# The two value products of a decoder block: stationary operands of 32 columns in four column tiles in place of 64 in two

## The reference, cut to what matters

```
# causal linear attention, q and k already turned and made positive by phi
num = einsum('bhd,bhde->bhe', q_t, sum over s <= t of k_s v_s)
den = max(einsum('bhd,bhd->bh', q_t, sum over s <= t of k_s), 1e-6)
y = num / den

# cross attention, Q = norm(x), K = V = ctx
attn = softmax(einsum('bhqd,bhkd->bhqk', Q, K) / sqrt(8))
context = einsum('bhqk,bhkd->bhqd', attn, V)
```

## Time and profile before

| | |
|---|---|
| runs, median (lowest to highest) | 1055.57 us (1054.49 to 1060.03), 3 runs |
| the profiled execution | 1064.24 us, its span 1062.0 us |
| TensorE: matmul busy, load busy | 863.1 us (81%), 695.8 us (66%) |
| VectorE, ScalarE, GpSimd busy | 730.3 us, 583.0 us, 598.8 us |
| mean granted TensorE clock | 0.926 of full speed |
| blocks of a_values, of b_values | 64 each, from 32.2 and 91.3 us on, the last at 597.9 and 666.4 us |

### The profile page before, as it was taken

How to read it: one execution, slowest core, us unless ns; L and a number is a source line. 1 busy time by engine, 2 the same in 40 slices (tenths; PEclk the granted TensorE clock), 3 DMA queues, 4 the chain that set the end, 5 groups by cost and what they waited for, 6 DMA issues and landing times.

```text
span 1062.0 us, 27434 instructions
## 1 busy us (share of the span) xinstructions
PE 863.1 (81%) x9293; PEld 695.8 (66%) x9294; DVE 730.3 (69%) x1980; ACT 583.0 (55%) x1116; POOL 598.8 (56%) x792
## 2 busy tenths in 40 slices
PE   4779989898888988898888875987988898888810
PEld 3567777677677776677766654876866676666610
DVE  2346768878887888787798986667555555555545
ACT  3567658667666667666766553532355555545410
POOL 4455435865766666676585665247066666665620
PEclk9789889999998999999999987898999999999965
DMA  9011011111101101102101103111122222222169
GB/s 250 2 41 41 2 41 44 32 49 46 55 24 51 52 22 51 51 22 60 46 29 52 59 14 120 34 37 33 31 72 76 69 70 72 68 68 65 52 182 298
DMA packets 92389, 65.96 MB, mean 62 GB/s; under 512 B 8943, under 2 KB 84472, under 8 KB 92288
## 3 DMA queue, kind: packets, MB, share of 16 engines
q1 hardware_dynamic: 75424, 43.46, 15.2%
q0 software_dynamic: 8416, 16.93, 4.8%
q10 hardware_dynamic: 8448, 4.20, 1.3%
HBM read 42.44 MB, written 22.56 MB: 61 GB/s over the span
## 4 chain that ended last, share of the span: by engine, by line
PE 41%; DVE 25%; issue 12%; ACT 10%; POOL 5%; DMA 3%; another core or an unknown queue 3%; SPq 1%; POOLq 0%; ACTq 0%; DVEq 0%
PE bank L802 6%; PE pair_x L784 4%; DVE mx L1318 3%; PE bank L700 3%; DMA Kblk<-mixed 3%; PE pair_x L688 2%; DVE b_xn L1302 2%; PE bank L460 2%; PE pair_y L688 2%; PE bank L792 2%; PE pair_x L519 2%; PE bank L538 2%; PE bank L630 2%; DVE Ex L1322 2%
## 5 line engine op out<-in xcount | busy, mean ns | idle before, releaser
L1216 POOL DMA_INDIRECT mixed<-f_y,f_x x135 | 133.7, 990 | 54.3 <-issue 31.8
L1135 POOL DMA_INDIRECT routed<-c_row,c_idx x128 | 127.5, 996 | 40.8 <-issue 40.8
L802 PE MATMUL bank<-Qblk,Am 128*128 x540 | 93.5, 296 | 30.1 <-DVE Am L1573 30.0
L802 PEld LDWEIGHTS bank<-Qblk,Am 128*128 128x128 f32 x540 | 71.0, 191 | 71.3 <-issue 71.1
L1067 POOL TENSOR_TENSOR tick<-minus_half 128x1 f32<-128x1 f32 x151 | 30.4, 201 | 138.2 <-DVE c_place L1403 72.4
L1092 POOL TENSOR_TENSOR Qblk<-qT,con 128x512 f32<-128x512 f32 x64 | 67.1, 1054 | 71.5 <-DVE qT L1270 71.2
L930 ACT COPY ExT<-pair_x 128x1024 f32<-128x1024 f32 x64 | 64.3, 1005 | 56.9 <-PE pair_x L613 44.2
L613 PE MATMUL pair_x<-con,Ex 128*128 128x128 f32 x512 | 72.4, 287 | 19.4 <-ACT Am L898 16.4
L1318 DVE TENSOR_REDUCE mx<-pair_y 128x16 f32<-128x1024 f32 x64 | 78.2, 1221 | 12.7 <-PE pair_y L599 11.7
L898 ACT ACTIVATE Am<-pair_x 128x1024 f32<-128x1024 f32 x64 | 64.8, 1013 | 40.1 <-remote 21.4
L613 PEld LDWEIGHTS pair_x<-con,Ex 128*128 128x128 f32 x512 | 57.7, 146 | 43.7 <-issue 42.3
(11 more groups left out here) (214 smaller groups left out, 2283.5 us busy)
## 6 DMA issues: line engine op xcount, KB each, us to landing
f_x<-routed SPq DMA_DIRECT2D x135, 65.0 KB
ctxD<-in_ctx SPq DMA_DIRECT2D x32, 256.0 KB, 4.2
ctxP<-in_ctx SPq DMA_DIRECT2D x16, 256.0 KB, 2.8
maskB<-in_mask_BxS_if SPq DMA_DIRECT2D x16, 256.0 KB, 4.1
Cblk<-mixed SPq DMA_DIRECT2D x16, 256.0 KB, 5.2
Kblk<-mixed SPq DMA_DIRECT2D x16, 256.0 KB, 6.1
block_out<-X ACTq DMA_DIRECT2D x16, 256.0 KB, 5.8
mixed<-f_y,f_x POOLq DMA_INDIRECT x135
```

The lines of the kernel that those rows point to most:

```text
L802: ins = pe.matmul(banks[F_O][:, 0:D], f_hT[:, u % 3, c * P:(c + 1) * P], wdn[:, bass.ds(e, 1), c, :].rearrange("p o d -> p (o d)"), start= ...
L1135: pool.indirect_dma_start(routed[:, :], bass.IndirectOffsetOnAxis(ap=c_idx[:, par, t, n:n + 1], axis=0), c_row[:, par, t, n, :], None, bou ...
L1216: pool.indirect_dma_start(mixed[:, :], bass.IndirectOffsetOnAxis(ap=f_x[:, u, D + 1:D + 2].bitcast(I32), axis=0), f_y[:, u, :], None, boun ...
```

## The change

In both value products each matmul is split in two by its queries: in place of 64 columns of the stationary operand the first takes the queries 0 to 31 and the second 32 to 63. Their outputs go to partitions 0 to 31, 32 to 63, 64 to 95 and 96 to 127 of the same bank, which are four column tiles of the array. The moving operand is the same 18 columns for both halves and is streamed for each. A block is now 32 matmuls in place of 16. The semaphores, the buffers, the order of everything else and all other engines stay as they are.

```diff
+TQ = T // 2
+QUARTERS = [(s, q) for s in range(2) for q in (0, TQ)]
...
                 for r in range(R):
-                    for s in range(2):
-                        ins = pe.matmul(num[s * T:(s + 1) * T, r // RH, :, r % RH, :], Am[:, j % 2, r // RH, s, r % RH, :],
+                    for s, q in QUARTERS:
+                        ins = pe.matmul(num[s * T + q:s * T + q + TQ, r // RH, :, r % RH, :],
+                                        Am[:, j % 2, r // RH, s, r % RH, q:q + TQ],
                                         Vblk[:, par, 2 * j + s, r, :, :], start=True, stop=True)
...
-                    for s in range(2):
-                        ins = pe.matmul(banks[B_O][s * T:(s + 1) * T, at:at + 2 * E9], ExT[:, j % 2, s, 2 * i + r, c, :],
+                    for s, q in QUARTERS:
+                        ins = pe.matmul(banks[B_O][s * T + q:s * T + q + TQ, at:at + 2 * E9],
+                                        ExT[:, j % 2, s, 2 * i + r, c, q:q + TQ],
                                         Cblk[:, par, 2 * j + s, i, c, r, :, :].rearrange("p q e -> p (q e)"),
                                         start=True, stop=True)
```

## The result

| kernel | median us (lowest to highest) | runs |
|---|---|---|
| before | 1056.66 (1054.49 to 1060.03) | 4 |
| changed | 1068.12 (1066.06 to 1073.84) | 4 |

The ratio is 1.0116 with an interval of 1.0088 to 1.0145: 1.2% slower. Forecast were 1046 us and a range to 1064 us, so the sign is wrong and the time outside the range. The profiled execution took 1070.1 us, its span is 1067.9 us.

The account below looks back on a forecast made before the run. TensorE and VectorE, neither full, were taken to hand work to each other, the chain running along TensorE's queue. 27 blocks at 0.38 us save 10 us: profiled 1064.2 to 1054, median 1055.6 to about 1046 us; range 1038 to 1064.

Parts of the forecast that it names:

- The length of a block: Value products: 16 rounds, 15 spacings of 31.5 ns plus 20 ns between tiles, 0.49 us for 0.87, saving 0.38 us.
- Rivals 3 and 4: Value blocks: only two loads at once, 0.11 us slower, chance 0.10; 25 ns floor between starts, 0.7 us slower, chance 0.07.
- 49 us of busy time, 10 on the path: TensorE: 128 blocks save 0.38 us each, 49 us busy; 27 blocks on the path give 10 us.
- the 27 blocks: Value blocks on the chain before 350 us, where TensorE leads; 0.38 us each, 10 us saved.
- So feeding costs between nothing and the whole gain. I take nothing: TensorE's instruction supply: 128 instructions a block take at most 1.0 us, need 0.5 us; cost taken as nothing.
- No semaphore, wait, buffer or DMA of data is added: Value products' first consumers on VectorE and ScalarE can only be let go earlier; no cost counted.
- Rival 5: All engines stand once a group behind dense TensorE instructions; one more stall in each of 10 groups, 1069 us, chance 0.05.
- 112 ns loads: Sign of being right: L538 and L630 with 4096 loads each of about 112 ns, 139 less 26.5.
- 45 us a line: Sign of being right: matmul busy time of L538 and L630 near 45 us each, in place of 72 and 75.
- TensorE at 815 us: Sign of being right: TensorE's total busy time near 815 us.
- shares below 2%: Sign of being right: L538 and L630 each fall below 2% of the chain.
- "Remote" waits well over 21 us: Sign of being wrong through longer or more frequent stalls: waits for semaphores whose matmuls had ended, 21.4 us before on ScalarE.

Follow-up runs that it names:

- half_32: Changed kernel, but from the second group on only queries 0 to 31, so 64 instructions a block; 1038.44 us, 0.9893 of the kernel before.
- before_again: The kernel before, unaltered, run once more on chip 7 for its trace; 1010.00 us.
- reverse: Kernel before with 32-column pieces only in the 40 blocks that run beside scatters; 1011.14 us, 1.0012 of the kernel before.
- selective: Kernel before with 32-column pieces only in the 88 blocks beside which no scatter runs; 998.30 us, 0.9888 of the kernel before.
- after_again: The changed kernel, unaltered, run once more on chip 7; 998.25 us, 0.9893 of the kernel before.
- no_scatter_32: Changed kernel without scatters in the routing, SyncE writing zeros instead; 950.06 us, 0.9417 of the kernel before.

## Why the prediction was wrong

- **The length of a block: right.** From the first to the last load's start it fell from 0.876 to 0.531 us (64 starts, 8.4 ns each); with the last load's end 0.64 us, inside the 0.60 to 0.65 given. In half_32, with two of the four column tiles in use, the 32 loads come in 16 pairs, 15 steps in 0.468 us, 31.2 ns each, against 31.5 worked out from the earlier trace rows (had the number of loads set the length, half as many would have taken half as long, 0.27 us). The 20 ns by which four tiles start apart are right for the first four loads (0, 7, 13 and 20 ns). But with four tiles the 15 steps take 0.498 us, 33 ns each, and the last four loads 33 ns: 0.531 us in place of 0.49. A block saves 0.345 us, not 0.38.
- **Rivals 3 and 4: refuted** by the same number. Two loads at once would have made 0.98 us, a floor of 25 ns 1.6 us. The floor of about 25 ns that the Trainium skill states in "TensorE: Matmul & The Clock Gate", section "Wait — 56ns, not 53.3ns?", does not hold over column tiles: starts over four of them came 8.4 ns apart. Its section "Packing small matmuls", with about 4 ns from tile to tile, is nearer, though the first four loads started 6.7 ns apart.
- **49 us of busy time, 10 on the path: right where nothing disturbs.** TensorE's busy time fell by 47.3 us (850.7 to 803.4), the median by 10.6 us. That the gain is won early, where TensorE leads, is borne out as well: at the block of the first attention that begins at 343 us in before_again the changed kernel is 9.5 us ahead, at the end of the span 10.7. That the sum fits so closely is in part luck: the 27 blocks were counted in the disturbed chain, and the gain came out in the calm setting. Reverse and selective split the blocks by the scatters and not by who leads, so their 0 and 10.5 us don't test this.
- **"So feeding costs between nothing and the whole gain. I take nothing", and "No semaphore, wait, buffer or DMA of data is added": here it failed.** The feeding itself was cheap (128 instructions in 0.64 us, 5 ns each). But beside GpSimd's scatters a denser run of instructions has a cost of its own, and I put no price on it. In the disturbed setting the change brought 72 us of stops on TensorE in place of most of the late semaphores. If the 10.6 us of gain are in it there too, 22 us stand against them (1068.1 less 1056.7, and 10.6); the two traces give 20.5 us for the stretch from the first scatter on.
- **Rival 5: the mechanism that decided, with a chance of 0.05.** Its price, 23 us less 10, gave 1069 us; measured were 1068.1. That the number fits is luck, for its working was another, and its place was only half right: not one more stop in each of 10 groups, but three to six inside each of 24 value blocks. It had been in view, 21 us of it on ScalarE alone, behind the densest run of TensorE instructions, and I knew that the change makes that run denser. The mistake was to take the stops for a curiosity, perhaps the recorder's, without looking for what stood beside each of them: they begin with the first scatter and not before.
- **What I said would show it:** 112 ns loads, yes; 45 us a line, no (55 and 68, stops included; 52 for L633 even in the calm setting, since the matmuls' mean stayed at 189 ns); TensorE at 815 us, no (844, and 803 in the calm setting); shares below 2%, no (2 and 3%) and yes in after_again. "Remote" waits well over 21 us as the sign of rival 5 was the wrong sign: they fell, and the stops showed as "issue".

**Open.** What makes a setting calm or disturbed: three chips were calm and two disturbed, beside the one of the first comparison, whose number isn't known, but none of the five was met twice, and all timed runs here were recorded in the same way, so chip, host and recording aren't told apart. Why completions of TensorE are late beside scatters: the runs show the two together, growing together, not the path between them. One candidate is the writing of the records of completion, which every run here had: the Trainium skill, "NOTIFIC — the notification-queue block", section "Overflow: three behaviours, one of which stalls the engine", says that in one of its settings a full queue of records stalls the engine that produces them. Which setting held here no run shows, and no run tests the candidate. `reverse` and the kernels without scatters never met a disturbed chip, so that stops vanish there with the scatters wasn't tried.

## What to carry to other kernels

A stationary operand split over four column tiles shortens a block bound by its loads, here by 0.345 of 0.876 us, and the gain on the path can be estimated from the chain as the blocks that stand in it whole (10 us forecast, 10.6 measured where nothing disturbed). But it doubles the instructions, and beside another engine's indirect DMAs that can cost more than it gives: look in the trace for stops on "issue" and for "remote" waits, see what runs beside each, and keep the larger pieces there. And compare a change of 1% on more than one chip, always beside the kernel before: here the time of one kernel moved by 4 to 5% from chip to chip, and the sign of the change with it.

## What the runs showed of the hardware

- **TensorE stops beside GpSimd's indirect scatters, in some settings.** In the disturbed one L630's semaphore came up to 3.7 us after the matmul's end, and in blocks of 64 loads TensorE stopped behind the 42nd to 46th and went on in steps of 0.7 us, mostly 3 to 6 loads each. The untouched experts' stage took 396 us there, and 346 in the calm one. Before the first scatter no semaphore was over 0.3 us late in either setting.
- **Single stops without any scatter beside them.** Without scatters and with 64-column pieces no block has a stop; with 32-column pieces 11 have one, up to 2.4 us (again 11 in the repeat, 8.8 us in all):

```profile
308.96 0.51 PEld L646 LDWEIGHTS bank<-Cblk,ExT 128*32 128x32 f32 x48 [0.17 <-issue]
...
311.76 0.31 PEld L646 LDWEIGHTS bank<-Cblk,ExT 128*32 128x32 f32 x16 [2.30 <-issue]
```

  (no_scatter_32; 10.3 us in all.) All 11 end 1.3 to 1.5 us after the end of a transfer on the queue that loads TensorE's instructions. So TensorE may here have outrun the supply of its instructions. That is a match of times, and no run has tested it; the amount itself may be an offset between the clocks of the two kinds of records.
